# Layer 0's probability transposes in a two-layer decoder: transpose mode or products with the identity

## The reference, cut to what matters

```python
# self, per sequence b and head h
scores = einsum('bhqd,bhkd->bhqk', Q, K) / dk ** 0.5        # dk = 16, causal
attn   = einsum('bhqk,bhkd->bhqd', softmax(scores), V)
out    = attn @ Wo
x = layernorm(x + out)
# cross: queries from x, keys and values from the context
ret = einsum('bhql,bhdl->bhdq', softmax(qk), vh)            # 8 heads of 32
x = layernorm(x + gamma * ret)
```

## Time and profile before

| what | us |
|---|---|
| runs before, median (lowest to highest) | 1012.95 (1008.82 to 1019.25) |
| the profiled execution's own time | 1011.51 |
| its span in the profile | 1009.6 |
| TensorE busy (matmuls) | 835.1 |
| VectorE busy | 599.2 |
| ScalarE busy | 438.6 |
| GpSimd busy | 421.3 |
| stream of `layer_0`, first score to last norm | 44.0 to 243.3 |

### The profile page before, as it was taken

How to read it: one execution, slowest core, us unless ns; L and a number is a source line. 1 busy time by engine, 2 the same in 40 slices (tenths; PEclk the granted TensorE clock), 3 DMA queues, 4 the chain that set the end, 5 groups by cost and what they waited for, 6 DMA issues and landing times. The chain is left out here.

```text
span 1009.6 us, 15980 instructions
## 1 busy us (share of the span) xinstructions
PE 835.1 (83%) x4870; PEld 500.4 (50%) x4870; DVE 599.2 (59%) x1901; ACT 438.6 (43%) x1418; POOL 421.3 (42%) x384
## 2 busy tenths in 40 slices
PE   7698899776766999799999997977973699999920
PEld 4465555543543443455555555863433455555510
DVE  3467646675584776588888883124665444334327
ACT  2477645352561000688888881001122255454412
POOL 4255434342260566366666661000000555666513
PEclk9869865887796999899999999998995599999965
DMA  9200000000000666200000000009701122222124
GB/s 331 109 1 2 1 1 1 0 1 1 1 1 15 160 166 170 86 2 1 1 2 2 2 1 1 1 0 413 213 1 42 37 63 66 75 63 70 53 70 138
DMA packets 29923, 59.61 MB, mean 59 GB/s; under 512 B 6433, under 2 KB 19117, under 8 KB 29104
## 3 DMA queue, kind: packets, MB, share of 16 engines
q1 hardware_dynamic: 20352, 41.01, 12.6%
q0 software_dynamic: 4608, 10.50, 3.4%
q10 hardware_dynamic: 4880, 7.08, 2.8%
HBM read 39.69 MB, written 8.39 MB: 48 GB/s over the span
## 5 line engine op out<-in xcount | busy, mean ns | idle before, releaser
L283 POOL TENSOR_TENSOR a_Pr<-a_Pr,a_rd 128x1024 f32<-128x1024 f32 x64 | 121.2, 1893 | 68.1 <-DVE a_rd L224 67.8
L256 ACT ACTIVATE a_Pr<-a_Sm,a_nm 128x257 f32<-128x257 f32 x256 | 127.3, 499 | 34.2 <-DVE a_nm L208 33.4
L801 POOL TENSOR_TENSOR l_Pr<-l_Pr,l_rd 128x256 f32<-128x256 f32 (+1 forms) x80 | 81.7, 1038 | 76.0 <-DVE l_rd L687 76.0
L208 DVE CUSTOM_DVE_ANT_0 a_Sm<-a_psS,table,NSK 128x256 f32<-128x256 f32 x256 | 107.9, 478 | 2.1 <-PE a_psS L157 1.8
L1510 POOL TENSOR_TENSOR ro_in_tile<-ro_in_tile,table 128x384 fp32r<-128x384 f32 x4 | 7.0, 1743 | 173.0 <-DVE ro_in_tile L1569 173.0
L157 PE MATMUL a_psS<-KT,QT 64*128 64x256 f32 x512 | 74.2, 410 | 5.7 <-DVE a_nm L208 3.9
L157 PEld LDWEIGHTS a_psS<-KT,QT 64*128 64x128 f32 x512 | 45.3, 190 | 57.9 <-issue 48.6
L1193 PE MATMUL p_ps<-p_XT,W 128*128 128x512 f32 x160 | 72.6, 612 | 0.8 <-ACT p_XT L1206 0.8
L1680 POOL DMA_INDIRECT pairs<-ex_y,ti_index x48 | 49.6, 1033 | 56.7 <-ACT ex_y L1785 44.5
L1223 DVE SCALAR_TENSOR_TENSOR p_T<-p_ps,BQK,table 128x512 f32<-128x512 f32 x80 | 56.4, 747 | 26.6 <-PE p_ps L1193 26.6
L1803 DVE TENSOR_TENSOR ex_a<-ex_psG,ex_sg 128x96 f32<-128x96 f32 x48 | 12.4, 258 | 100.6 <-ACT ex_sg L1773 82.7
(11 more groups left out here) (260 smaller groups left out, 1922.3 us busy)
## 6 DMA issues: line engine op xcount, KB each, us to landing
w_in<-in_w_in SPq DMA_DIRECT2D x1, 6144.0 KB, 18.1
QT<-p_E SPq DMA_DIRECT2D x64, 64.0 KB, 2.1
QT<-p_E ACTq DMA_DIRECT2D x64, 64.0 KB, 2.1
c_in<-in_c_in SPq DMA_DIRECT2D x1, 4096.0 KB, 28.6
co_G<-pairs SPq DMA_DIRECT2D x8, 512.0 KB, 7.2
W<-in_w SPq DMA_DIRECT2D x1, 3072.0 KB, 12.9
w_out<-in_w_out SPq DMA_DIRECT2D x1, 3072.0 KB, 42.8
KT<-p_E SPq DMA_DIRECT2D x32, 64.0 KB, 2.1
```

The costliest lines, as they stand in the source:

```text
L208: nc.vector.tensor_tensor_reduce(out=Sm[:, t % 2, n, 0:S], in0=psS[:, 2 * (t % 2) + n // 2, n % 2, :], in1=mask[:, n % 2, :], scale=-scale ...
L256: nc.scalar.activation(Pr[:, t % 4, n, :], src, ACT.Exp, bias=nm[:, t % 2, n:n + 1], scale=scale if mask is None else -1.0, accum_out=den[ ...
L283: pool.tensor_tensor(p, p, rd[:, t % 2, :].unsqueeze(2).to_broadcast([P, 4, S]), ALU.mult).then_inc(normed, 1)
L801: last = pool.tensor_tensor(p, p, r.unsqueeze(2).to_broadcast([P, n, n_keys]), ALU.mult)
```

## The change

In `turn` of `layer_0` each `transpose` becomes an ordinary product with the same operands: the block of probabilities is the stationary operand, the identity the moving one, and the result is the same transposed block at the same place in `l0_psT`. Order, waits, semaphores and buffers stay as they are; the transposes of all other stages stay as they are too. Each of the 320 blocks becomes two MATMUL records with two weight loads.

```diff
                 for u in range(2):
                     need(pe, s["copied_a" if u == 0 else "copied_v"], t)
                     for qt, kt, at in blocks:
-                        last = nc.tensor.transpose(psT[:, u, at:at + P],
-                                                   Pr[:, t % 4, 2 * u + qt, kt * P:(kt + 1) * P], c["ident"])
+                        p = Pr[:, t % 4, 2 * u + qt, kt * P:(kt + 1) * P]
+                        last = nc.tensor.matmul(psT[:, u, at:at + P], p, c["ident"], start=True, stop=True)
                     last.then_inc(s["turned"], 1)
```

## The result

The changed kernel took 1018.65 us (median of 20 runs, 1015.91 to 1021.91), the kernel before 1015.19 us (20 runs, 1004.90 to 1026.63): ratio 1.0056, 95% interval 1.0038 to 1.0075. It is half a per cent slower, where the prediction had it half a per cent faster, at 1008.3 us. Both are within 1%, but the sign was missed. A second comparison gave 1016.39 us against 1021.25, ratio 0.9969 (0.9934 to 1.0003). The changed kernel hardly differs between the two; the kernel before does.

What follows compares the result with a forecast made beforehand. It took TensorE to bound half-clock self steps, and the exponentials between ScalarE and VectorE to pace full-clock steps. Stretch terms summed to -3.2 us from the profiled 1011.5, giving 1008.3 us; range 999.0 to 1031.0.

Steps and rivals of the forecast that it cites:

- What a block costs: Layer 0's turns: a block gets 0.117 us dearer at full clock, a six-block turn 0.69, an eight-block turn 0.93.
- The clock rises and holds in the self part: Layer 0's self steps: full-array products lift TensorE to full clock from about 57 us and keep it there.
- 45.0 to 67.1, -0.7: Stream start: two turns at half clock cost 1.3 us more each, the last three steps reach full clock; -0.7 us.
- 67.1 to 116.2, +5.9: Self steps already at full clock: 16 turns add 11.0 us, of which idle time absorbs 5.1; +5.9 us.
- 116.2 to 134.8, -4.6: Five self steps at half clock, 18.6 us, become full-clock steps of 2.81 us each; -4.6 us.
- 134.8 to 152.8, -1.5: Self part: an output and step gain from full clock, three turns cost 0.69 us each, idle absorbs 1.3; -1.5 us.
- 152.8 to 186.7, -2.5: Into the cross part: four steps fall to 4.24 us, one with the output takes 13.4; 31.4 of 33.9, -2.5 us.
- 186.7 to 229.0, +0.2: Nine cross steps: TensorE's 3.6 us fit the 4.24 us pace of the exponentials; +0.2 us, bounds -1 and +5.
- 229.0 to 243.3, 0: The stream's drain: the last two turns cost 0.93 us more each, offset by records at full clock; 0 us.
- the second rival: Clock rises in the self part but drops in the cross part: +6.9 us, about 1018.4 us; chance 15%.
- The third rival: More comes back: idle time of 67.1 to 116.2 absorbs more, feed-forward starts at full clock; 1000.4 us; chance 12%.
- The first rival: The clock doesn't rise and every half-clock stretch of the stream stays: +40.8 us, about 1052 us; chance 15%.

Runs made afterwards that it cites:

- e1: Against the kernel before, every block in layer 0's turns is transposed twice in transpose mode, no products: 1016.66 us, ratio 1.0026.
- e5: Against the kernel before, each slot's scores are computed twice and blocks stay transposes: 1047.49 us, ratio 1.0304.
- e3: Against the kernel before, ordinary products in the 16 cross slots only, transposes in the self slots: 1030.41 us, ratio 1.0084.
- e7: Against the kernel before, blocks stay transposes and two products nobody reads follow the mix in 12 cross-part steps: 1024.02 us, ratio 0.9917.
- e12: The changed kernel measured once more beside new runs of the kernel before: 1016.39 us, ratio 0.9969.

## Why the prediction was wrong

Its sum was -3.2 us; the two profiles differ by +7.8 in the stream, and the medians by +3.5 (+5.7 by the ratio). By its own steps:

- *What a block costs* (0.117 us at full clock): right. A turn of six blocks grew by 0.73 us (1.53 for 0.80) where 0.69 was said; of eight by 0.97 (1.99, 221.54 to 223.53, for 1.02) where 0.93 was said. Two records a block, 640 in all, as forecast.
- *The clock rises and holds in the self part*: right in what happens (0.67, then 1.00 three times). As to why, the prediction named two suspects, transposes and narrow scores, and said that its rows could not separate them. e1 acquits the transposes, and e5 leaves the narrow scores. "Full-array products lift the clock where the mixture of transposes and narrow products doesn't" is too strong even for the profile of before: there the clock rose at 67.0 in that very mixture.
- *45.0 to 67.1, -0.7*: +0.4 from the first score to the seventh step; that the clock came at 58.8 and not at 57 accounts for most of it.
- *67.1 to 116.2, +5.9*: measured 56.2 for 49.1, +7.1. The step was right as a mechanism and undersized: not 5.1 but 4.6 of the idle 7.2 us were absorbed (16 turns x 0.73 = 11.7, less 7.1).
- *116.2 to 134.8, -4.6*: -3.8. *134.8 to 152.8, -1.5*: -1.0. The self steps are 2.75 and 2.96, mean 2.86, where 2.81 was said.
- *152.8 to 186.7, -2.5*: 34.0 for 33.9, nothing gained, though its clock is 0.90 where it was 0.60. Two clock falls (164.6 and 174.9, 3.4 us each) fell into turns of sixteen records; the four steps that were to take 17.0 us took 18.6.
- *186.7 to 229.0, +0.2*: this is the step that failed most. It measured +4.8. That TensorE's 3.6 us "fit into the 4.24 of the ring" is true of a plain step at full clock (4.25, with 0.57 idle). What failed is that it was carried over to steps at half clock. The clock fell at 195.3 and 209.0 in spite of the products, and at half clock a cross step takes 6.61 us with products (209.40 to 216.01) and 4.92 with transposes (191.77 to 196.69 before): the turn that was to be free is on the path with 1.7 us. Against their counterparts the two steps in which it fell grew by 0.3 and 2.4 us, where the prediction had half-clock steps gain. A smaller part is size alone: the two steps with a norm grew by 0.7 and 1.0 at full clock, where 0.6 each was said. The other steps make up the last 0.4 or so. The bound given, +5, was about the measured value.
- *229.0 to 243.3, 0*: +0.3.

These errors add up to 11 us, of which 7.5 lie in the last three stretches. Nearest to what happened is the second rival, to which the prediction gave 15%. That its price, 1018.4 us, is within 0.3 us of the median is luck: the first five stretches came out 6.2 us worse than it assumed (+2.8 for -3.4), the last two 5.2 better (+5.1 for +10.3), since the clock's share there is 0.86 and 0.97 and not half. The third rival didn't come: the full-clock stretch took +7.1, and the feed-forward stage again began at half clock (250.0 to 263.6). Of the signs that were to show the forecast right, the clock of the self part, the 640 records, the self steps and the plain cross steps came true; a clock near 1.00 until 230 us (0.90 and 0.86) and the stream's end near 240 (250.5) did not, and one of the signs against it, a cross step over 6 us, was there. The first rival (no rise, 1052) is refuted for products.

One thing outside the sum. The profiled execution of before was taken for the kernel: it had a self part of 109.8 us, and e3 and e7 show the same instructions in 122. Against 122 the change gains 10 us in the self part, against 109.8 it loses 2; none of its 30 runs shows a group as far from the rest as before's, and such a change must be measured against both groups.

A turn of products costs nearly twice a turn of transposes (1.53 for 0.80 us). The Trainium skill ("Perfetto Trace Analysis", "Transposes") says to use the transpose, and as to price the trace agrees. The Trainium skill ("TensorE: Matmul & The Clock Gate", "Terms") has the transpose mode four times faster for float32, which the trace doesn't show. Transposes in the place of products held the clock at 1.00 for 133 us in e1. The Trainium skill ("TensorE: Matmul & The Clock Gate", Part 4) says that transpose mode doesn't count as busy in the same way and that the full clock doesn't engage for it; for the float32 transposes of this kernel the measurement is otherwise.

## What to carry to other kernels

Where TensorE is always busy and still at half clock, look at how much of the array its records fill before blaming their mode; a few full-array records a step can be worth several times their time (here 32 x 0.11 = 3.5 us of them for a median of 1006.85 us, where in the same comparison the change has 1016.39 and before 1021.25). In a stage that waits for other engines a dearer operation is free only in the steps with room for it: price it at half clock too, and in the steps where the engine behind it has more to do. Look at whether the kernel before has more than one profile before taking one for its time.

## What the runs showed of the hardware that was not expected

- Transposes of float32 hold TensorE's clock as well as ordinary products: 133 us at 1.00 in e1, with twelve records of each self step in transpose mode.
- TensorE busy for 98% of 68 us got 1.2 GHz throughout, where 32-row scores took more than half of each step (69.77 to 72.64 of the 4.92 us from 67.72; e5).
- The order in which the clock came up at the start goes roughly with the dose of full-array work: 53.9 to 58.8 us with all self blocks doubled or as products, 61.1 to 70.5 with a third of them, 75.6 with one, 67.0, 93.6 and 95.6 with none, 111.9 with the scores doubled instead. With no dose it varies by 28.6 us between executions of the same instructions.
- The clock's falls in the cross part of the changed kernel came at the same four places in both of its profiles, within 0.1 us (e12).
- A second transpose of one block in six, 0.11 us a step, gave 1006.85 us (four runs); products in all six cost 0.73 us a step and gave 1016.39 us in the same comparison.
